# Sixteen float32 matmuls with an unread result in front of eight TensorE steps of the first unit

## What is computed

```python
# attention, 16 heads of 16
scores = jnp.where(causal, -inf, q @ k.T / 4)
vals, idx = jax.lax.top_k(scores, 32)         # all else is masked
y = softmax(masked) @ v @ Wo.T + bo
x = _layernorm(x + y)
# experts: proj_in (8, 512, 256), proj_out (8, 256, 512)
h = relu(einsum('edi,bsi->bsed', proj_in, x))
o = einsum('eid,bsed->bsei', proj_out, h)
x = _layernorm(x + einsum('bsei,bse->bsi', o, gate))
# ffn: Hadamard transform, 4-bit activations, ternary weights
x = _layernorm(x + ffn(x))
```

## Time and profile before

| | |
|---|---|
| median of 3 runs | 622.53 us (621.35 to 623.42) |
| the profiled execution | 624.53 us |
| its span, first to last instruction | 622.7 us |
| mean granted clock of TensorE | 0.941 |
| TensorE busy | 553.3 us, 89% |
| VectorE busy | 477.5 us, 77% |
| ScalarE busy | 387.2 us, 62% |
| GpSimd busy | 344.3 us, 55% |

### The profile page before, as it was taken

The page is one execution under the profiler, slowest core; times in us unless marked ns, Lnnn a source line. Parts: engine busy times, 40 slices in busy tenths (PEclk is TensorE's granted clock), DMA queues, the critical chain, the costliest instruction groups (busy, mean ns, idle before and its releaser), DMA issues. The chain is left out here.

```text
span 622.7 us, 20334 instructions
## 1 busy us (share of the span) xinstructions
PE 553.3 (89%) x7156; PEld 478.9 (77%) x7156; DVE 477.5 (77%) x2995; ACT 387.2 (62%) x909; POOL 344.3 (55%) x336
## 2 busy tenths in 40 slices
PE   4565648999899999999999999999999999989942
PEld 3454537898788888888888888888888888878831
DVE  1898879986889978898879887988789898553213
ACT  3688558666567566766667576766575767646520
POOL 2488556753447464754556455655554656555831
PEclk9568578999999999999999999999999999999985
DMA  7244220001000200002000100020001000000000
GB/s 234 78 146 136 86 103 2 3 17 37 3 2 3 64 8 2 3 3 69 3 1 21 53 3 2 3 70 1 3 3 53 3 3 1 19 0 3 18 0 17
DMA packets 20021, 19.88 MB, mean 32 GB/s; under 512 B 1744, under 2 KB 17872, under 8 KB 19920
## 3 DMA queue, kind: packets, MB, share of 16 engines
q1 hardware_dynamic: 19920, 18.59, 9.6%
HBM read 16.49 MB, written 2.10 MB: 30 GB/s over the span
## 5 line engine op out<-in xcount | busy, mean ns | idle before, releaser
L462 POOL TENSOR_TENSOR h_lo<-h_raw,h_hi 128x512 f16<-128x512 f32 x128 | 149.5, 1169 | 158.9 <-ACT h_raw L580 158.2
L768 PE MATMUL ps_o<-w_hi,h_lo 128*128 128x256 f16 x512 | 139.8, 273 | 4.3 <-POOL h_lo L462 3.1
L752 PE MATMUL ps_z<-x1t_hi,w_lo 128*128 128x256 f16 x512 | 140.5, 274 | 0.6 <-DVE x1t_lo L910 0.6
L752 PE MATMUL ps_z<-x1t_lo,w_hi 128*128 128x256 f16 x512 | 140.3, 274 | 0.0
L752 PE MATMUL ps_z<-x1t_hi,w_hi 128*128 128x256 f16 x512 | 140.3, 274 | 0.0
L768 PE MATMUL ps_o<-w_hi,h_hi 128*128 128x256 f16 x512 | 139.5, 273 | 0.0
L768 PE MATMUL ps_o<-w_lo,h_hi 128*128 128x256 f16 x512 | 139.5, 273 | 0.0
L854 DVE MATCH_REPLACE8 taken<-next,taken 128x48 f32<-128x48 f32 (+2 forms) x576 | 127.6, 233 | 0.2
L576 ACT ACTIVATE h_hi<-ps_z 128x512 f16<-128x512 f32 x128 | 75.9, 593 | 57.9 <-PE ps_z L752 57.0
L849 DVE MAX8 next<-taken 128x8 f32<-128x48 f32 (+2 forms) x576 | 95.9, 235 | 0.1
L483 POOL TENSOR_TENSOR acc<-go_sb,acc 128x512 f32<-128x512 f32 x56 | 71.2, 1271 | 36.4 <-ACT go_sb L590 36.2
(11 more groups left out here) (106 smaller groups left out, 993.5 us busy)
## 6 DMA issues: line engine op xcount, KB each, us to landing
w_raw<-in_w1t SPq DMA_DIRECT2D x8, 512.0 KB, 3.8
w_raw<-in_w2t SPq DMA_DIRECT2D x8, 512.0 KB, 5.0
xt_sb<-in_xt SPq DMA_DIRECT2D x8, 256.0 KB, 3.3
x_sb<-in_x SPq DMA_DIRECT2D x8, 256.0 KB, 3.1
out<-out_sb SPq DMA_DIRECT2D x8, 256.0 KB, 2.1
ctx_sb<-in_ctx_w SPq DMA_DIRECT2D x8, 128.0 KB, 2.3
itok_sb<-in_itok SPq DMA_DIRECT2D x8, 128.0 KB, 2.5
wq_sb<-in_wqt SPq DMA_DIRECT2D x1, 256.0 KB, 2.9
```

Of the source, the lines that this page charges most:

```text
L462: nc.gpsimd.tensor_tensor(h_lo[:, e % 2, 2 * z:2 * z + 2, :], h_raw[:, z, :, :], h_hi[:, e % 2, 2 * z:2 * z + 2, :], ALU.subtract)\
L752: last = pe.matmul(ps_z[z][:, d * UT:(d + 1) * UT], w[:, e, c, at:at + P], x[:, c, :], start=n == 0, stop=n == len(terms) - 1)
L768: last = pe.matmul(ps_o[e % 2][:, b * D:(b + 1) * D], h[:, e % 2, c, b * SEQ:(b + 1) * SEQ], w[:, e, c, :], start=n == 0, stop=n == len(te ...
```

## The change

It adds a table, `WARMED`, of eight TensorE steps with a count each, and a function `keep_warm`. Ahead of each of the eight steps, in the first unit alone, TensorE now issues so many matmuls. Each takes the identity (128 x 128) as weights and wq_sb seen as 128 x 512, in float32, and writes the 512 columns of ps_z1. They wait for nothing and raise no semaphore, and nothing reads what they write. The call stands ahead of the step's own waits.

```diff
+WARMED = {("turn_probs", 1, 0): 3, ("turn_probs", 2, 0): 3, ("turn_probs", 3, 0): 3, ("attend", 3): 1, ("turn_o",): 1,
+          ("out_proj",): 1, ("turn_x1",): 3, ("L1", 0, 0): 1}
...
+            def keep_warm(count):
+
+                for _ in range(count):
+                    pe.matmul(ps_z[1][:, :], ident[:, :], wq_sb[:, :, :].rearrange("p c n -> p (c n)"),
+                              start=True, stop=True)
+
             def step(name, v, *args):
+                if v == 0 and (name, *args) in WARMED:
+                    keep_warm(WARMED[(name, *args)])
                 if name in MISC:
                     take_misc(name, v, *args)
```

## The result

| | before | after |
|---|---|---|
| median, six executions each | 622.35 us (621.35 to 623.42) | 625.89 us (624.50 to 626.66) |
| ratio | | 1.0057 (1.0041 to 1.0073) |
| the profiled execution, its span | 624.53, 622.7 us | 625.84, 624.0 us |
| mean granted clock | 0.941 | 0.957 |
| TensorE busy | 553.3 us | 563.3 us |

The change makes the kernel 3.5 us slower, with a higher mean clock. The forecast was 625.3 us, 2.8 later than before. The two profiled spans differ by only 1.3 us, and this is the first thing to explain: the profile of before on which the prediction rests is of an execution that took 624.5 us, above all six in the table.

A forecast was written before the change was run, and what follows sets the result against it. TensorE was taken as the bound from 98 to 603 us, so only L1's start and the low clock after it mattered. 3.0 + 1.0 - 1.25 = 2.8 us on the 622.5 median gave 625.3, range 620.0 to 628.3.

The forecast's parts named there:

- The first group: Three matmuls ahead of turn_probs(1,0), where TensorE has no gap: VectorE 2.75 us late, by way of ScalarE's queue.
- The second group: Three matmuls ahead of turn_probs(2,0), no gap: w_sum late, VectorE's lateness goes from 2.75 to about 3.9 us.
- VectorE has no slack against it: At w_sum behind turn_probs(2,0): VectorE had already waited 0.80 us, so w_sum's delay to 61.0 reaches it.
- The third and the clock behind it: Three ahead of turn_probs(3,0) are free in a 5.52 us gap; clock falls between 68 and 72 us; 0.5 to 0.7 won.
- attend(3), v, out_proj: Matmul ahead of attend(3) costs 1.79 us; copy_v 3.8 late; out_proj's vanished wait leaves 3.0 late at ln1_stats.
- turn_x1 and L1: Three ahead of turn_x1 free, clock falls anyway; one ahead of L1 costs 1.0 us; clock rising sooner wins 1.25.
- any shift of that point: A shift of the first expert matmul's start (L752, 94.05 us) goes to the end nearly one for one.
- the forecast's own rule: Low-clock time in L1 costs half of itself: 2.0 us before, 0.75 with the change.
- 1.0 - 1.25: At L1: the added matmul costs 1.0 us, and the clock rising sooner wins 1.25 us.
- Rival A: The clock holds at both gaps, ahead of turn_probs(3,0) and turn_x1: 3.5 us faster, 619.0; chance 0.15.

The follow-up runs named there:

- early_only: The changed kernel with only the three matmuls ahead of turn_probs(1,0) and the three ahead of turn_probs(2,0): 625.03 us, ratio 1.0054 to before.
- first_only: The changed kernel with only the three matmuls ahead of turn_probs(1,0): 624.33 us, ratio 1.0034 to before.
- second profile of before: The kernel before, unchanged, profiled once more: 620.99 us, span 619.2 us.
- without_early: The changed kernel less the matmuls ahead of turn_probs(1,0) and turn_probs(2,0), ten left: 622.42 us, ratio 1.0006 to before.
- no_attend: The kernel without_early less the one matmul ahead of attend(3), nine left: 621.60 us, ratio 0.9977 to before.
- six_only: The changed kernel with only six matmuls, all ahead of turn_probs(3,0): 622.76 us, ratio 0.9998 to before.
- bridge_l2: The kernel bridge plus two matmuls into ps_o1 in the first L2's wait for VectorE: 621.45 us, ratio 0.9968 to before.
- bridge: The changed kernel with only six matmuls ahead of turn_probs(3,0), one ahead of w_sum(6), five ahead of turn_x1: 622.16 us, ratio 0.9994 to before.

## Why the prediction was right

**The first group: right, and it is the larger part of the change.** The working was 2.75 us, with ends of 2 and 3.8. Between keep 1 and keep 2 the profiles show 2.0 (early_only), 2.9 (the change) and 3.0 us (first_only); the time of first_only is 2.1 us over before (its interval is 1.2 to 3.0). The way named, over ScalarE's queue to VectorE, is the one in the rows: ScalarE waits 5.07 instead of 2.03 us. One place was missed on it: VectorE also waits at w_sum of the fourth expert (2.28 us at 50.64), which takes most of the delay ahead of `keep`.

**The second group: mis-sized.** The term was 1.15 us; it measured 0.24 to 0.45 between keep 2 and keep 3, and 0.5 us in time, not clear of noise. The step that failed is "VectorE has no slack against it". The wait did grow by as much as forecast, but the operations behind it became shorter by 0.8 us, since they no longer ran beside x_plus_bo.

**The third and the clock behind it: right in kind.** turn_probs(3,0) came at 70.47 (69.9 forecast, of which 1.06 is this execution's own start), and the clock fell once more, at 72.5 (68 to 72 forecast).

**attend(3), v, out_proj: mis-sized, and read from one execution.** The working went from 3.9 late at keep 3 to 3.0 at ln1_stats, 0.9 won. In the two first profiles it is 2.0 won (22.80 against 20.81 up to ln1_apply): v ran wholly at the full clock (1.99 us), and copy_v came 2.6 us later than before, 1.06 of which is the execution's own start, where 3.8 was forecast with ends of 2.8 and 5.0. But the second profile of before needs 20.27 for the same stretch. In the time, the ten later matmuls win nothing: without_early is at 1.0006. The prediction took the low clock of one execution (10.25 us busy) for the kernel's own state. It was one draw of several, and it left less to be won than the rows seemed to say.

**turn_x1 and L1: wrong, and it mattered little.** The forecast was that the clock would fall ahead of turn_x1, that L1 starts at 97 to 99 us, and that this start, plus half of its low-clock time, sets the end. The clock held, L1 started at 96.01 at the full clock, and 4.0 us of low-clock time went. By the forecast's own rule that would have been 2.0 us won. Instead the first L2 waited 1.79 us for w_step: the bound behind L1 is VectorE's queue. What failed is the first part of the prediction, that "any shift of that point", L1's start, goes to the end; it is the start of ln1_apply that does, plus 533.6 to 534.9 us in all 14 profiles: 534.7 or 534.8 where L1 ran low for 4 us, and 533.6 or 533.7 where the clock held through L1 and behind it. The forecast for this place was 1.0 - 1.25 = -0.25; it measured -1.1, of which 0.3 is the start of L2 and 0.8 the scores behind it, ahead of which TensorE's gap went from 1.08 to 0.31 us; why it did stays open.

**In sum:** 2.1 for the first group, 0.5 for the second, 0.4 for the ten others (their ratios alone) give 3.0 us against 3.5 measured. The forecast's terms for the three are 2.75, 1.15 and -1.15, in sum 2.8. So the sign came from the first group, whose way was worked out rightly; that the sum is so near is luck, since 1.3 us too much in the first two stand against 1.6 us too little in the third. Rival A, that the clock holds at both gaps, nearly came about in the profile of after, whose clock fell once after 59 us, for 3.4 us. From keep 3 to the end this execution is 3.1 us shorter than the first profile of before and only 0.5 shorter than the second, so an execution of before without the change had most of this already.

## What to carry to other kernels

An unread matmul is free only where the engine's next step really waits; read the gap ahead of that very step in the trace, and if there is none the filler delays the step in full. What comes of it depends on who waits for the step, which may be two engines on: at turn_probs(1,0) 2 to 3 us of it reached VectorE, at turn_probs(2,0) only 0.2 to 0.5. To hold the clock surely, a filler has to reach to the moment when the awaited data comes. With three matmuls in a gap that takes six, 2.3 to 2.6 us stay idle, and the clock fell close to that gap in some executions (no_attend at 66.7 and again at 90.6 us) and held over it in others (at turn_x1 in the change and in without_early). And it has to do so at every gap in a row: the first gap filled by itself won nothing (six_only, 0.9998), and all gaps together won 0.3%. The Trainium skill, page "TensorE: Matmul & The Clock Gate", section "Why this matters for your kernels", advises to leave no long idle gaps between bursts; bridge_l2 agrees with that (0.9968), and the change (1.0057) shows that the fillers must not stand ahead of work that is ready. And where stretches at the low clock decide, one profile is one draw: take two before pricing such a stretch.

## What the runs showed of the hardware

One and the same program had its clock changes at other places from one execution to the next: the v projection of before ran once at the low and once at the full clock (3.78 and 1.99 us), and its times spread over 0.8%. In bridge the clock went low amid dense matmuls, at 99.1 us, just behind 3.4 us with 1.64 us of work; a fall may thus be paid by work that had no part in the gap. Four float32 transposes take 1.06 to 1.12 us at the low and 0.60 to 0.66 at the full clock, so they follow the clock like the rest. An added float32 matmul of 512 columns took 0.87 to 0.88 us in a row at the full clock (5.28 us for six in bridge_l2 and in six_only, there from 62.80 to 68.08), as worked out from the projections. And small int32 operations of VectorE, 0.17 us long by themselves, took up to 0.65 us beside GpSimd's x_plus_bo and ended just behind one of its two pieces, in 12 of 14 profiles.
